# A two-layer autoencoder in split float32: recombining adds by accumulating DMAs, a first and last step in pieces, and one weight sum by a DMA in half of the steps of four

## The reference

```python
# x (512, 2, 1024), W_enc (2, 1024, 4096), W_dec (2, 4096, 1024), all float32
f = jax.nn.relu(jnp.einsum('bld,ldf->bf', x, W_enc) + b_enc)     # 512 x 4096, contraction over 2 x 1024
x_hat = jnp.einsum('bf,lfd->bld', f, W_dec) + b_dec              # 512 x 2 x 1024, contraction over 4096
```

## Time and profile before

| | us |
|---|---|
| median of 3 runs (693.22 to 693.76) | 693.49 |
| the profiled execution | 693.06 |
| its span, first to last instruction | 691.3 |

### The profile page before, as it was taken

The page is one execution under the profiler, slowest core; times in us unless marked ns, Lnnn a source line. Parts: engine busy times, 40 slices in busy tenths (PEclk is TensorE's granted clock), DMA queues, the critical chain, the costliest instruction groups (busy, mean ns, idle before and its releaser), DMA issues.

```text
span 691.3 us, 7987 instructions
## 1 busy us (share of the span) xinstructions
PE 649.4 (94%) x2888; PEld 527.4 (76%) x2888; DVE 599.0 (87%) x773; ACT 339.2 (49%) x423; POOL 0.7 (0%) x6
## 2 busy tenths in 40 slices
PE   2989999999999999999999999998979998989996
PEld 0867888888878888888888888876757876767885
DVE  4999989879999858579994999999999999999844
ACT  3455335354564444556566665454444453454452
POOL 0000000000000000000000000000000000000000
PEclk9999999999999999999999999999999999999999
DMA  8966675665566564647455665654545554445524
GB/s 300 306 186 187 199 223 182 203 191 165 157 199 204 179 197 138 197 137 224 141 191 175 185 211 185 206 189 136 183 146 159 183 182 140 159 143 181 191 101 181
DMA packets 66518, 126.90 MB, mean 184 GB/s; under 512 B 4784, under 2 KB 4784, under 8 KB 66480
## 3 DMA queue, kind: packets, MB, share of 16 engines
q1 hardware_dynamic: 66480, 126.40, 56.9%
HBM read 122.18 MB, written 4.19 MB: 183 GB/s over the span
## 4 chain that ended last, share of the span: by engine, by line
PE 68%; DVE 25%; issue 4%; DMA 1%; ACT 1%; SPq 0%; DVEq 0%; ACTq 0%
PE sums L502 22%; PE sums L504 22%; PE sums L503 22%; DVE w_split L321 9%; DVE w_raw L321 5%; DVE place L321 5%; DVE forms L321 3%; PE sums L514 3%; DVE s_sum L321 3%; DMA w_raw<-w_enc 1%; ACT place L270 0%; ACT place L282 0%; ACT forms L250 0%; ACT w_split L232 0%; ACT forms L248 0%
## 5 line engine op out<-in xcount | busy, mean ns | idle before, releaser
L502 PE MATMUL sums<-w_split,forms 128*128 128x512 f32 x896 | 357.4, 399 | 34.8 <-DVE w_split L321 26.9
L232 ACT CAST w_split<-w_raw 128x1024 fp32r<-128x1024 f32 (+1 forms) x256 | 240.2, 945 | 297.1 <-PE sums L504 219.2
L504 PE MATMUL sums<-w_split,forms 128*128 128x512 f32 x896 | 352.0, 393 | 0.0
L503 PE MATMUL sums<-w_split,forms 128*128 128x512 f32 x896 | 351.8, 393 | 0.0
L321 DVE TENSOR_TENSOR w_split<-w_raw,w_split 128x1024 fp32r<-128x1024 f32 (+1 forms) x256 | 268.8, 1086 | 61.1 <-ACT w_split L232 61.0
L502 PEld LDWEIGHTS sums<-w_split,forms 128*128 128x128 f32 x896 | 169.8, 189 | 81.1 <-issue 29.6
L504 PEld LDWEIGHTS sums<-w_split,forms 128*128 128x128 f32 x896 | 169.8, 190 | 36.1
L503 PEld LDWEIGHTS sums<-w_split,forms 128*128 128x128 f32 x896 | 170.1, 190 | 33.5
L321 DVE TENSOR_TENSOR w_raw<-w_raw 128x512 f32<-128x512 f32 x256 | 176.2, 688 | 9.2 <-DMA w_raw<-w_enc 4.8
L321 DVE TENSOR_TENSOR place<-place,sums 128x1024 f32<-128x1024 f32 x28 | 32.5, 1214 | 8.1 <-PE sums L504 8.1
L321 DVE TENSOR_TENSOR place<-place 128x1024 f32<-128x1024 f32 x28 | 33.1, 1218 | 0.0
(11 more groups left out here) (16 smaller groups left out, 47.7 us busy)
## 6 DMA issues: line engine op xcount, KB each, us to landing
w_raw<-w_enc SPq DMA_DIRECT2D x96, 512.0 KB, 5.0
w_raw<-w_dec SPq DMA_DIRECT2D x96, 512.0 KB, 4.5
w_raw<-w_enc SPq DMA_DIRECT2D x32, 256.0 KB, 3.0
w_raw<-w_dec SPq DMA_DIRECT2D x32, 256.0 KB, 2.7
place<-xT SPq DMA_DIRECT2D x9, 512.0 KB, 7.6
outT<-place SPq DMA_DIRECT2D x16, 256.0 KB, 2.2
b_enc_sb<-b_enc SPq DMA_DIRECT2D x1, 16.0 KB, 8.8
b_dec_sb<-b_dec SPq DMA_DIRECT2D x1, 8.0 KB, 9.3
```

The costliest lines, as they stand in the source:

```text
L232: nc.scalar.copy(split(s, q, 0), w_pos(s, 2 * q, n)).then_inc(hi_done, 1)
L502: nc.tensor.matmul(out, v_hi, w_hi, start=k == 0, stop=False)
L503: nc.tensor.matmul(out, v_lo, w_hi, start=False, stop=False)
L504: last = nc.tensor.matmul(out, v_hi, w_lo, start=False, stop=k == PAIRS - 1)
```

## The change

Six things are changed.

- The recombination of `dec2` and `dec3`: five of the seven adds of a chunk become DMAs of 512 KB from SBUF to SBUF with an add at the destination, issued by Pool (`fold_in`, at the steps k = 4, 5 and 6 of the chunk behind). VectorE keeps two: y21 from banks 4 and 5, and V from banks 6 and 7 less U2. ScalarE's copies get a sign, so that all accumulations are additions.
- T1 by such a DMA of 256 KB (Pool) in 32 of the 64 steps of four (`by_dma`): steps 4 to 7, 26 to 31, all of chunks 11 and 13, the first six of chunk 12. Pool waits for the step's weights; ScalarE and VectorE wait for the DMA (`w_summed`).
- In front of such a step VectorE makes T2 and T4 behind the lows of the step before, not ahead of them.
- Step 0 is loaded in six DMAs of 256 KB, and its high and low parts are made position by position, so that each product can start when its own parts are there.
- In the last chunk the first products of steps 126 and 127 go ahead of the second ones and these ahead of the third; the last product of step 127 stands between the transposes of tiles 3 and 4.
- `WARM` is 12.

```diff
...
-    WARM = 8
+    WARM = 12
...
+    FOLDS = {"enc1": 0, "enc2": 0, "dec1": 0, "dec2": 5, "dec3": 5, "dec4": 0}
+    FOLDED = [16 * sum(FOLDS[ch[1]] for ch in CHUNKS[:n]) for n in range(len(CHUNKS) + 1)]
...
+    def by_dma(s):
+        n, k = s // PAIRS, s % PAIRS
+        if not FOUR[s]:
+            return False
+        return n == 0 and k >= 4 or n in (11, 13) or n == 12 and k < 6 or n == 3 and k >= 2
+
+    def dma_sums(s):
+        return 16 * sum(1 for t in range(s % RAW, s + 1, RAW) if by_dma(t))
+
     def dve_sums_of(s):
+        if by_dma(s):
+            return 2
         return 3 if FOUR[s] else 1
...
-            for s in range(RAW):
+
+            first_x, first_w = whole(X_PLACE[0]), slice(0, C)
+            sp.dma_start(first_x[:, 0, :], x_pairs[:, 0, 0, :]).then_inc(piece_loaded[0], 16)
+            sp.dma_start(w_pos(0, 0), w_enc[0:P, 0, first_w]).then_inc(piece_loaded[1], 16)
+            sp.dma_start(first_x[:, 1, :], x_pairs[:, 0, 1, :]).then_inc(x_loaded[0], 16)
+            sp.dma_start(w_pos(0, 1), w_enc[0:P, 1, first_w]).then_inc(piece_loaded[2], 16)
+            low = slice(PAIRS * P, (PAIRS + 1) * P)
+            sp.dma_start(w_pos(0, 3), w_enc[low, 1, first_w]).then_inc(w_loaded[0], 16)
+            sp.dma_start(w_pos(0, 2), w_enc[low, 0, first_w]).then_inc(w_loaded[0], 16)
+            for s in range(1, RAW):
...
+            def fold(dst, src):
+                pool.dma_start(whole(dst), whole(src), accum_op=ALU.add).then_inc(folded, 16)
+
+            def fold_in(n, part):
+                y11, y12, y21, y22 = out_place(n)
+                if part == 0:
+                    pool.wait_ge(summed, SUMMED[n + 1])
+                    fold(U3, V_PLACE)
+                    fold(y21, V_PLACE)
+                elif part == 1:
+                    pool.wait_ge(copied, COPIED[n + 1])
+                    fold(y11, U2)
+                else:
+                    pool.wait_ge(folded, FOLDED[n] + 48)
+                    fold(y12, U3)
+                    fold(y22, U3)
+
+            for s in range(STEPS):
+                n, k = s // PAIRS, s % PAIRS
+                if by_dma(s):
+                    pool.wait_ge(w_loaded[s % RAW], 32 * (s // RAW + 1))
+                    pool.dma_start(w_pos(s, 1), w_pos(s, 0),
+                                   accum_op=ALU.add).then_inc(w_summed[s % RAW], 16)
+                if n and k in (4, 5, 6) and FOLDS[CHUNKS[n - 1][1]]:
+                    fold_in(n - 1, k - 4)
+
...
-                act.wait_ge(w_sums_done, W_SUMS[s + 1])
+                if by_dma(s):
+                    act.wait_ge(w_summed[s % RAW], dma_sums(s))
+                if q or not by_dma(s):
+                    act.wait_ge(w_sums_done, W_SUMS[s + 1])
...
-                nc.scalar.copy(whole(dst), banks(p)).then_inc(copied, 1)
+                negative = kind != "enc1" and dst in (y22, U3)
+                nc.scalar.activation(whole(dst), banks(p), ACT.Copy,
+                                     scale=-1.0 if negative else 1.0).then_inc(copied, 1)
...
+                if by_dma(s):
+                    dve.wait_ge(w_summed[s % RAW], dma_sums(s))
+                else:
+                    dst, src = (1, 0) if FOUR[s] else (0, 2)
+                    add(w_pos(s, dst), w_pos(s, dst), w_pos(s, src)).then_inc(w_sums_done, 1)
+                    if not FOUR[s]:
+                        return
+                    first += 1
+                    dve.wait_ge(w_sums_done, first)
+                add(w_pos(s, 3), w_pos(s, 3), w_pos(s, 1)).then_inc(w_sums_done, 1)
                 dve.wait_ge(w_sums_done, first + 1)
-                add(w_pos(s, 3), w_pos(s, 3), w_pos(s, 1)).then_inc(w_sums_done, 1)
-                dve.wait_ge(w_sums_done, first + 2)
                 add(w_pos(s, 2), w_pos(s, 2), w_pos(s, 3)).then_inc(w_sums_done, 1)
...
                     first = kind == "dec2"
                     if k == 1:
                         dve.wait_ge(copied, COPIED[n])
+                        dve.wait_ge(folded, FOLDED[n])
                         dve.wait_ge(multiplied, ready + 3)
-                        op = add(y21, y22 if first else y21, banks(2))
-                    elif k == 2:
+                        op = add(y21, y22 if first else y21, banks(2), sub)
+                    else:
                         dve.wait_ge(copied, COPIED[n + 1])
-                        op = add(y11, y11, u2)
-                    elif k == 3:
                         dve.wait_ge(multiplied, ready + 4)
-                        op = add(u2, banks(3), u2, sub)
-                    elif k == 4:
-                        dve.wait_ge(summed, before + 3)
-                        op = add(u3, u2, u3, sub)
-                    elif k == 5:
-                        op = add(y21, y21, u2, sub)
-                    elif k == 6:
-                        dve.wait_ge(summed, before + 4)
-                        op = add(y12, u3, whole(out_place(n - 2)[1]) if first else y12)
-                    else:
-                        op = add(y22, u3, y22, sub if first else ALU.add)
+                        op = add(v, banks(3), u2, sub)
                 op.then_inc(summed, 1)
...
+            at, kh = pair_place(0, 0)
+            dve.wait_ge(begun_hi, 1)
+            add(forms[:, 0, 1, 0, :], place[:, at, :], forms[:, 0, 0, 0, :].bitcast(F32),
+                ALU.subtract).then_inc(begun_lo, 1)
+            dve.wait_ge(begun_hi, 2)
+            add(split(0, 0, 1)[:, 0:C], w_pos(0, 0), split(0, 0, 0)[:, 0:C].bitcast(F32),
+                ALU.subtract).then_inc(begun_lo, 1)
             form_sums(0, 0)
-            w_sums(0)
-            form_lo_direct(0, 0)
+            dve.wait_ge(piece_loaded[2], 16)
+            add(w_pos(0, 1), w_pos(0, 1), w_pos(0, 0)).then_inc(w_sums_done, 1)
+            dve.wait_ge(form_hi, 1)
+            add(forms[:, 0, 1, 2, :], place[:, at + kh + 1, :], forms[:, 0, 0, 2, :].bitcast(F32),
+                ALU.subtract)
             form_lo_sums(0, 0)
+            dve.wait_ge(hi_done, 1)
+            add(split(0, 0, 1)[:, C:2 * C], w_pos(0, 1), split(0, 0, 0)[:, C:2 * C].bitcast(F32),
+                ALU.subtract).then_inc(lo_done, 1)
+            dve.wait_ge(w_loaded[0], 32)
+            dve.wait_ge(w_sums_done, 1)
+            add(w_pos(0, 3), w_pos(0, 3), w_pos(0, 1)).then_inc(w_sums_done, 1)
+            dve.wait_ge(w_sums_done, 2)
+            add(w_pos(0, 2), w_pos(0, 2), w_pos(0, 3)).then_inc(w_sums_done, 1)
...
-                if s + 1 < STEPS:
+                if s == 0:
+                    lo(s, 1)
+                late = s + 1 < STEPS and by_dma(s + 1)
+                if s + 1 < STEPS and not late:
                     w_sums(s + 1)
-                lo(s, 0)
+                if s:
+                    lo(s, 0)
                 if k == 1 and kind in ("dec2", "dec3"):
                     take_out(n - 1, 2)
-                    take_out(n - 1, 3)
                 if k == 1 and kind == "enc1":
                     take_out(n - 1, 1)
-                lo(s, 1)
+                if s:
+                    lo(s, 1)
+                if late:
+                    w_sums(s + 1)
                 for r, i in FORMS_AT.get(s, ()):
                     form_lo_direct(r, i)
                     form_lo_sums(r, i)
                 if k == 1 and kind == "enc1":
                     take_out(n - 1, 2)
                     take_out(n - 1, 3)
-                if k in (2, 3) and kind in ("dec2", "dec3"):
-                    take_out(n - 1, 2 * k)
-                    take_out(n - 1, 2 * k + 1)
...
-                multiply(s)
+                if s < STEPS - 2:
+                    multiply(s, range(4 if FOUR[s] else 3))
+                elif s == STEPS - 2:
+
+                    multiply(s, [0])
+                    multiply(s + 1, [0])
...
+            multiply(STEPS - 2, [1])
+            multiply(STEPS - 1, [1])
+            multiply(STEPS - 2, [2])
             for j in range(8):
+                if j == 4:
+                    multiply(STEPS - 1, [2])
                 pe.wait_ge(summed, SUMMED[n] + (3 if j < 4 else 4))
...
```

More of the change, by code:

```diff
@@ L58, in autoencoder_kernel @@
              "dec1": [(True, 1), (True, 2), (True, 3)],
-             "dec2": [(True, 1), (True, 2), (False, 1), (False, 3)],
-             "dec3": [(True, 1), (True, 2), (False, 1), (False, 3)]}
+             "dec2": [(True, 1), (True, 2), (False, 1), (False, 2)],
+             "dec3": [(True, 1), (True, 2), (False, 1), (False, 2)]}
+    def by_dma(s):
[5 more added lines that the diff above has]
+        return 16 * sum(1 for t in range(s % RAW, s + 1, RAW) if by_dma(t))
     def dve_sums_of(s):
+        if by_dma(s):
+            return 2
         return 3 if FOUR[s] else 1
@@ L103, in autoencoder_kernel @@
         w_loaded = [sem(f"w_loaded{s}") for s in range(RAW)]
+        w_summed = [sem(f"w_summed{s}") for s in range(RAW)]
         x_loaded = [sem(f"x_loaded{i}") for i in range(PAIRS + 1)]
```

(49 more changed lines are left out.)

5 lines of the change are left out of this document (4 added, 1 removed).

## The result

| | before | after |
|---|---|---|
| median (before 693.22 to 695.36, after 687.44 to 690.27) | 693.49 | 688.86 |
| profiled execution, its span | 693.06, 691.3 | 687.44, 685.1 |
| step 7 starts (chunk 0) | 62.16 | 57.38 |
| first matmul of chunk 11 | 456.0 | 451.4 |
| first matmul of chunk 15 | 645.1 | 638.0 |

The ratio is 0.9929 (95%: 0.9908 to 0.9949): 0.7% faster, clear of the spread, but by 4.6 us in the median where 32.8 were forecast. The profiled execution was the quickest of five; its span fell by 6.2 us.

A forecast was written before the change was run, and what follows sets the result against it. TensorE bounds the kernel, except VectorE in chunks 11 to 14 and losses at the ends. Gains of 24.3 + 7.0 + 0.6 + 0.9 = 32.8 us give 660.7 us; 655 to 667 had chance 0.60, 655 to 690 eight in ten.

The forecast's parts named there:

- VectorE's load and what it is worth: Chunks 11 to 14: VectorE relieved, TensorE becomes the limit, gaining 24.3 of 25.8 us lost (bounds 17 to 25.8).
- The price of an accumulating DMA: T1s and folds in the DMA queues, chunks 11 to 14: costed at nothing, range 0 to 10 us.
- m: Factor on an accumulating DMA's queue time for also reading its destination; at 2, 9.8 us too much until chunk 13's end.
- 10 us of lead: Weight loads, asked for 21.7 us ahead, were to keep about 10 us after landing, T1, T2, T4 and a high.
- Rival A: DMA queues become the limit in chunks 11 to 13, m at 2 to 2.8: 670 to about 693 us; chance 0.20.
- Rival B: Chunks 11 to 13: accumulating DMA costs three copies or more, 701 us at m = 3, slower from 2.8; chance 0.11.
- The chunk's head: Bank 6 and 7's add (V) comes at 458.4 us, before TensorE asks at 460.1; before the change it came at 461.6.
- Chunk 0: Start: step 0 in pieces (3.4 us), four T1s by DMA (2.8) and order (1.4); taken as 7.0, bounds 4 and 8.5.
- the doubt that was named: Chunk 0's gain was doubted for the clock, TensorE pausing some 4 us between the first two steps' parts.
- Chunk 3: T1 by DMA there removes waits for lows where forms overload VectorE a little: 0.6 us (0 to 1).
- Tail: After the last steps: reordered products let adds, transposes and stores start earlier, gaining 0.9 us (-0.5 to 1.5).
- Four of eight go out earlier: Tail: four of the eight final stores leave earlier, the rest takes 2.8 us.

The follow-up runs named there:

- e9: Changed kernel with the add left out of all Pool DMAs, which only copy (T1 and five adds a chunk not computed): 663.68 us, ratio 0.9568.
- e1: Changed kernel with all T1 sums back on VectorE, the folds still accumulating DMAs: 676.74 us, ratio 0.9761.
- e6: e1 with the three sums of steps 90, 98 and 106 behind the lows of the step before: 674.02 us, ratio 0.9715.
- e4: Kernel before with the change's two ends alone (start and tail), no accumulating DMA: 692.01 us, ratio 0.9984.
- e7: e1 with each fold cut into two DMAs of 2 KB a partition: 674.88 us, ratio 0.9728.
- e2: Changed kernel with the seven recombining adds back on VectorE, T1 still by DMA: 678.99 us, ratio 0.9787.
- e3: Changed kernel with the same bytes by DMA but one fold a step at k = 3 to 7: 683.94 us, ratio 0.9860.
- e5: Changed kernel with the last chunk's fourth add behind VectorE's tiles 1 and 3: 687.12 us, ratio 0.9901.
- e8: Changed kernel with e1 (T1 by DMA in steps 4 to 8 alone), e5, e6 and e7 joined: 668.83 us, ratio 0.9656.
- e10: e8 with T1 by DMA in three more steps, 95, 96 and 97: 671.34 us, ratio 0.9681.
- e11: e8 with 34 matmuls on zeros in TensorE's pauses of steps 0 and 1: 668.19 us, ratio 0.9638.
- e12: e11 with folds as single 512 KB DMAs, one a step at k = 3 to 7: 669.70 us, ratio 0.9663.

## Why the prediction was wrong, step by step

- **VectorE's load and what it is worth: right.** 24.3 us were forecast for chunks 11 to 14 (bounds 17 to 25.8). With VectorE relieved and nothing else in the way, e9 gives 189.0 - 163.4 = 25.6.
- **The price of an accumulating DMA: bounded right, and its worth misjudged. This is the step that failed.** The sum left m open between 1 and 2 and beyond; it is 2.07 (e9). The Trainium skill says of a reduce-scatter's add (Collectives: The Full Stack, "The bandwidth ceiling") that it needs two source reads and so runs at about half a copy's rate; for this add from SBUF to SBUF the trace agrees, with 2.07. The need by the prediction's sum at m = 2 is 47.6 + 44.8 + 47.6 + 30.8 = 170.8 us; the profile has 0.93 x 186.6 = 173.5. What was wrong is "up to m = 2 I cost them at nothing", with 10 us of lead set against an excess of 9.8. That lead was worked out with landings of half-empty queues, 4.7 us and as much for T1. At step 94 the landing took 15.2 us and T1 6.9: with 2.5 for T2, T4 and a high, more than the 21.7 us by which the weights are asked for ahead. Nor is the lead a store to be drawn on: a step's weights are asked for when the lows of four steps earlier are done, so a late step makes a later request late, and full stretches stand beside ones in which the queues have little to do:

```profile
513.40:529.40 16.00, 16.00 (x72) 13.25 (x71) 12.12 (x17) 6.25 (x8) 1.75 (x2) 1.00 1.07 289
592.00:608.00 16.00, 13.77 (x61) 11.07 (x60) 15.76 (x24) 10.32 (x15) 1.29 (x3) 1.00 0.44 153
```

 Since the share reads up to 1.07 where the queues are full, the 0.93 over the whole stretch leaves some 23 of the 186.6 us unused (an estimate, with 1.06 as full), and what they moved would have filled about 164 us, hardly more than TensorE's 163.1. So the adds left the queues no room, and the loss came from time that the queues couldn't use rather than from a sum far over TensorE's. The cost was 23.3 us, not 0 to 10.
- **Rival A was what happened**, at its lower end in m and far over its price (661 to 670 for m = 2). Its price had the excess and no idle queue time. The measured 688.86 lies in the outer range of 655 to 690, but by A's own sum only m = 2.7 would give it, so that agreement is luck. Rival B's mechanism was the same with m too high; its point of 2.8 should have stood nearer to 2: at 2.07 all but 2.4 us of 25.6 were gone.
- **The chunk's head: half right.** V was to come 1.7 us before TensorE asks. In the changed kernel it still comes late, but TensorE's wait for it is down to 0.1 to 0.6 us in chunks 11 to 13, from 1.4 to 3.7; in e9 it is gone. What hangs on that order with T1 on VectorE is 1.6 us of the stretch (e1 and e6).
- **Chunk 0: 4.8 instead of 7.0**, within its bounds. Step 7 starts at 59.1 to 60.3 us in the kernels with step 0 in pieces and no T1 by DMA (e1, e4, e6, e7), and at 56.6 to 59.5 in those with the T1s of steps 4 to 7 by DMA and the same order (the changed kernel, e2, e3, e5, e9). By the means, the pieces gave 2.5 of 3.4 us, and the T1s with the order 1.8 of 4.2. Two things stand behind that. The order's gain was counted for step 6 and 7, but the three sums of step 8, still on VectorE, stand ahead of the low of step 7:

```profile
53.96 2.14 DVE L394 TENSOR_TENSOR w_raw<-w_raw 128x512 f32<-128x512 f32 x3
56.02 1.22 DVE L394 TENSOR_TENSOR w_split<-w_raw,w_split 128x1024 fp32r<-128x1024 f32 x1
```

 TensorE waits 1.16 us for that low; with step 8's T1 by DMA (e8, e10) there is no wait at step 7. And the clock fell, the doubt that was named: with zeros in the pauses as well, e11 and e12 get step 7 at 55.3 and 55.1, where 55.2 was forecast. Without the zeros e8 and e10 have 57.0 and 58.2. Since step 7 varies that much between kernels with the same start, 4.8 is one reading, and which of the two weighed more isn't shown.
- **Chunk 3: 0 instead of 0.6.** The waits at steps 34 and 35 are there with T1 by DMA and without (e1), 0.6 and 0.4 us, as in the kernel before: T1 is not what they wait for. That the local order is behind them is not shown.
- **Tail: -0.9 instead of +0.9.** "Four of eight go out earlier" failed: two of the four tiles are VectorE's, and its queue has the last add ahead of them (e5).

## What to carry to other kernels

When work moves from a full engine to the DMA queues, price it in queue time with the add counted twice, and compare it per stage with the time of the engine that should become the limit; here, by the prediction's sum at m = 2, a need of 0.85 of that time (36.7 of 43.4 us, e8) left most of the gain, 0.94 (41.0, e10's chunk 12) gained nothing more, and at 1.03 and 1.10 (44.8 and 47.6, chunks 12 and 11 of the change) most of it was gone. A prefetch whose request depends on the consumer is no reserve against a lasting excess, and its lead has to be worked out with the landing times of full queues. Each half of the move was worth more than the whole, so try the halves.

## Not expected of the hardware

- The factor of 2.07 in queue time for an accumulating DMA from SBUF to SBUF, against a plain one of the same bytes (102.8 to 49.6 us for 18.88 MB), and a median of 9.8 us to land 512 KB beside loads (6.8 without the add: e9's median).
- Cutting a fold's rows from 4 KB to 2 KB raised the queue time of the same bytes from 55.4 to 60.2 us and didn't shorten the stretch beside it (e7).
- A pause of 2.05 us at the head of chunk 15 was followed by 3.4 us at the lower clock in e1; one of 2.06 us at the same place in the changed kernel wasn't.
